# All attention products of an audio tower layer on VectorE, none on GpSimd

## The reference

```python
h = einsum('bnp,dp->bnd', patches, W) + b            # 640 tokens x 512
x = layernorm(h)
q, k, v = x@Wq.T, x@Wk.T, x@Wv.T                     # 16 heads of 32; q, k rotated by position
scores = q k^T / sqrt(32), causal
heavy  = top 10% of the column sums of softmax(scores)   # 1 key of 10
scores = where(heavy | band of width 1, scores, -inf)
h = h + (softmax(scores) @ v) @ Wo.T
x = layernorm(h)
h = h + (silu(x@Wgate.T) * (x@Wup.T)) @ Wdown.T          # inner width 2048
```

## Time and profile before

| what | value |
|---|---|
| median of 3 runs | 337.02 us (336.95 to 338.04) |
| span of the profiled execution | 334.9 us, first to last instruction |
| the median above that span | 2.1 us |
| TensorE busy | 280.9 us (84%) |
| VectorE busy | 210.3 us (63%) |
| GpSimd busy | 157.8 us (47%) |
| mean granted clock of TensorE | 0.946 of full speed (2.4 GHz) |

### The profile page before, as it was taken

One profiled execution on the slowest core, in us unless ns is written; L12 is line 12 of the kernel. 1 busy time (PEld: TensorE's weight loads), 2 busy tenths in 40 slices (PEclk: granted clock), 3 DMA queues, 4 the chain that ended last, 5 costly groups with the idle time before them and its releaser, 6 DMA issues.

```text
span 334.9 us, 4376 instructions
## 1 busy us (share of the span) xinstructions
PE 280.9 (84%) x1528; PEld 247.4 (74%) x1528; DVE 210.3 (63%) x307; ACT 111.8 (33%) x185; POOL 157.8 (47%) x107
## 2 busy tenths in 40 slices
PE   2889689957696898949579998999999999999930
PEld 1468468847585797848469997889999999999920
DVE  4687999999569998598599266554342342342130
ACT  3650110072001544543821033344443443443200
POOL 0656784147847599574599005614223223223100
PEclk9999979989787899989979999999999999999995
DMA  7904777427442054433222202326442433410002
GB/s 251 389 0 95 203 246 179 127 46 206 104 119 94 2 190 145 156 136 125 94 94 94 96 0 80 105 100 225 154 156 94 143 139 94 140 48 0 0 24 70
DMA packets 17602, 39.89 MB, mean 119 GB/s; under 512 B 1908, under 2 KB 10356, under 8 KB 17076
## 3 DMA queue, kind: packets, MB, share of 16 engines
q1 hardware_dynamic: 17588, 39.71, 37.3%
HBM read 34.46 MB, written 5.24 MB: 119 GB/s over the span
## 4 chain that ended last, share of the span: by engine, by line
PE 46%; DVE 28%; issue 9%; ACT 4%; DMA 4%; POOL 3%; SPq 2%; DVEq 0%; ACTq 0%; POOLq 0%
PE ps L201 40%; DVE prod L236 5%; PE ps L1008 4%; DVE hT L847 3%; DVE sm L701 3%; DVE xn L664 2%; POOL wvo L363 2%; DVE pr L729 2%; DVE rstd L661 2%; DVE gu L841 1%; SPq L269 1%; DMA bias_raw<-b_tok 1%; DVE prod L240 1%; DMA regroup<-rot 1%; DVE xT L671 1%
## 5 line engine op out<-in xcount | busy, mean ns | idle before, releaser
L201 PE MATMUL ps<-xT,wgu 128*128 128x256 f32 (+1 forms) x768 | 123.6, 319 | 1.9 <-DVE xT L671 1.8
L201 PEld LDWEIGHTS ps<-xT,wgu 128*128 128x128 f32 x768 | 120.6, 197 | 5.3 <-DVE xT L671 2.5
L363 POOL TENSOR_TENSOR wd<-stage,wd 128x512 fp32r<-128x512 f32 x32 | 52.1, 1631 | 79.2 <-ACT wd L476 79.2
L201 PE MATMUL ps<-wd,hT 128*128 128x512 f32 x240 | 62.7, 403 | 14.6 <-DVE hT L847 13.2
L201 PEld LDWEIGHTS ps<-wd,hT 128*128 128x128 f32 x240 | 44.3, 190 | 24.2 <-DVE hT L847 14.7
L841 DVE TENSOR_TENSOR gu<-silu,ps 128x256 f32<-128x256 f32 (+1 forms) x32 | 15.5, 484 | 62.1 <-PE ps L201 44.2
L363 POOL TENSOR_TENSOR wgu<-stage,wgu 128x1024 fp32r<-128x1024 f32 x16 | 40.0, 2498 | 13.3 <-ACT wgu L476 13.3
L476 ACT ACTIVATE wgu<-stage 128x1024 fp32r<-128x1024 f32 x32 | 33.7, 1055 | 22.8 <-PE ps L201 20.3
L201 PE MATMUL ps<-wvo,xT 128*128 128x512 f32 x120 | 33.6, 439 | 5.1 <-issue 3.2
L847 DVE TENSOR_TENSOR hT<-gu,hT 128x256 fp32r<-128x256 f32 (+1 forms) x32 | 24.3, 759 | 20.5 <-ACT hT L476 20.5
L201 PEld LDWEIGHTS ps<-wvo,xT 128*128 128x128 f32 x120 | 25.2, 215 | 11.9 <-issue 3.3
(11 more groups left out here) (76 smaller groups left out, 270.8 us busy)
## 6 DMA issues: line engine op xcount, KB each, us to landing
stage<-w_ffn SPq DMA_DIRECT2D x32, 768.0 KB, 4.3
regroup<-rot SPq DMA_DIRECT2D x40, 64.0 KB, 2.4
regroup<-v_out SPq DMA_DIRECT2D x20, 64.0 KB, 1.9
stage<-w_k SPq DMA_DIRECT2D x1, 1024.0 KB, 6.4
stage<-w_q SPq DMA_DIRECT2D x1, 1024.0 KB, 8.9
stage<-w_v SPq DMA_DIRECT2D x1, 1024.0 KB, 10.9
stage<-w_o SPq DMA_DIRECT2D x1, 1024.0 KB, 12.9
k_all<-regroup SPq DMA_DIRECT2D x4, 256.0 KB, 2.8
```

The source lines that it names most:

```text
L201: ins = pe.matmul(dst, lhs[a], rhs[b], start=first and n == 0, stop=last and n == 2)
L363: pool.tensor_tensor(dst, src, f32(hi), ALU.subtract).then_inc(done, 1)
```

## The change

The two lists go; every key and value product is made by VectorE, and GpSimd's program has none. The semaphores `score_pool` and `pv_pool` go, and with them VectorE's waits on them. On VectorE the key products (0, 5), (0, 7), (0, 9), (1, 5), (1, 7) are made right before their reductions. The value products are put into its `values` calls: (0, 9) and (0, 8) after (0, 0), ahead of the rotations; (1, 8) after (1, 9), (1, 7) before (1, 6), (1, 4) after (1, 5). TensorE waits on one counter for all of them.

```diff
-POOL_SCORES = [(0, 5), (0, 7), (0, 9), (1, 5), (1, 7)]
-POOL_VALUES = [(0, 9), (0, 8), (1, 8), (1, 7), (1, 4)]
...
@@ GpSimd
             lo_vo(0, 3)
-            scores(0, 5)
-            scores(0, 7)
-            scores(0, 9)
             rotation_sum(6)
             for k in range(KT):
                 lo_vo(1, k)
-            values(0, 9)
             rotation_sum(7)
             rotation_sum(8)
-            values(0, 8)
             rotation_sum(9)
...
             lo_down(0, 0, 0)
-            scores(1, 5)
-            scores(1, 7)
             lo_block(2, 2)
...
-            values(1, 8)
-            values(1, 7)
-            values(1, 4)
             lo_block(12, 0)
@@ VectorE
             def scores(g, i):
-                if (g, i) in POOL_SCORES:
-                    dve.wait_ge(score_pool, POOL_SCORES.index((g, i)) + 1)
-                else:
-                    rotated(dve, g, i)
-                    step(key_products(dve, g, i))
+                rotated(dve, g, i)
+                step(key_products(dve, g, i))
...
-                    if g:
-                        dve.wait_ge(pv_pool, value_number((g - 1, 8)))
...
-            values(0, 5, 4, 3, 2, 1, 0)
+            values(0, 5, 4, 3, 2, 1, 0, 9, 8)
...
-            values(1, 9)
+            values(1, 9, 8)
             up_product(A, 10, 0)
-            values(1, 6)
+            values(1, 7, 6)
             low_product(A, 10, 0)
-            values(1, 5, 3)
+            values(1, 5, 4, 3)
@@ TensorE
-                    pe.wait_ge(pv_pool if (g, i) in POOL_VALUES else pv_dve, value_number((g, i)))
+                    pe.wait_ge(pv_dve, VALUES.index((g, i)) + 1)
```

More of the change, by code:

```diff
@@ L182, in audio_tower @@
         project_mm, rot_read, rot_sum, v_sb = sem("project_mm"), sem("rot_read"), sem("rot_sum"), sem("v_sb")
-        score_pool, score_sum = sem("score_pool"), sem("score_sum")
+        score_sum = sem("score_sum")
         exp_in, exp_out = sem("exp_in"), sem("exp_out")
-        probs, pv_dve, pv_pool, pv_mm = sem("probs"), sem("pv_dve"), sem("pv_pool"), sem("pv_mm")
+        probs, pv_dve, pv_mm = sem("probs"), sem("pv_dve"), sem("pv_mm")
         attn_hi, attn_lo, wo_mm = sem("attn_hi"), sem("attn_lo"), sem("wo_mm")
@@ L242, in value_products @@
                                      repeated(pr[:, i, :, 0:i + 1].rearrange("p h j -> p j h"), 3, HD), ALU.mult)
-        def value_number(item):
-            return sum((k in POOL_VALUES) == (item in POOL_VALUES) for k in VALUES[:VALUES.index(item) + 1])
         def stage_count(p, i, slot):
@@ L386, in rotation_sum @@
                 pool.tensor_tensor(rot[:, n % ROT], rot_cos[:, n % 2], rot_sin[:, n % 2], ALU.add).then_inc(rot_sum, 1)
[L388 to L397, removed]
             def lo_gu(i, slot):
```

## The result

The changed kernel takes 346.33 us (median of 4 executions, 344.73 to 346.95), the kernel before 337.27 (4 executions): a ratio of 1.029, 95% interval 1.024 to 1.034. The span of its profiled execution is 344.6 us against 334.9, 9.7 us longer. The forecast was 345.0.

What follows compares the result with a forecast made beforehand. Bound by a chain of TensorE (46%) and VectorE (28%), with VectorE and GpSimd taking turns in SBUF. 1.5 + 3.8 + 1.0 + 1.7 = 8.0 us on the 334.9 span gives 342.9, median 345.0; range 338.3 to 348.0.

Steps and rivals of the forecast that it cites:

- Group 0: Scores and values ahead of the rotations, made by VectorE alone: first softmax reduction 1.1 us later, `project_out` 1.5 us later.
- Scores of group 1: Products (1, 5) and (1, 7) among GpSimd's low halves in steps 1 to 4: `low_product(3)` 3.8 us later, bounds 0 to 5.
- the two branches: Order at `low_product(2)`, asked within 0.02 us of GpSimd's `lo_gu(5)`: VectorE first, 3.8 us later; GpSimd first, 3.9.
- the rest a turn more: Steps 1 to 4: beyond 2.2 us of own time, (1, 5) and (1, 7) each wait one more turn; 3.8 in all.
- Softmaxes of group 1: Stretch after the group's scores: order and turns of the engines stay as they were, adding nothing.
- Values of group 1: Products (1, 8) and (1, 7) now on VectorE: `low_product(10)` 1.0 us later; (1, 4) free under the value sums.
- The lost turn: Rival at 174.6: GpSimd goes first, so `low_product(10)` is 3.3 us later, not 1.0; total 347.3 us, chance 0.22.
- The clock: TensorE's stall ahead of `down(10)` becomes 2.6 us, its clock falls: 1.7 us more, bounds 0 and 1.7.
- The plain exchange: Rival: new turns cost no more than old, group 1 evens out, only group 0's 1.5 us stays; 338.5 us, chance 0.18.
- The faster one: Rival, steps 1 to 4: low halves fall under VectorE's reductions, 3.3 us of waits go; 335.2 us, chance 0.08.
- it doesn't show: Rival: low clock stretches end where they did and eat the first 1.5 us, the rest evens out; 337.0 us, chance 0.06.
- nothing comes back: Group 1 scores, positions 0 to 3: freed of GpSimd's products, VectorE then waits for the `silu` of step 0; 0 us gained.

Runs made afterwards that it cites:

- the cut of the holding time: GpSimd's gate and up low halves, blocks 2 to 15, first pass, cut from 1024 to 128 columns in both kernels: spans 324.9 us (changed), 322.0 (before).

## Why the prediction was right, and where it wasn't

Counted from the first key product, the forecast's steps against the trace:

| step | forecast | measured |
|---|---|---|
| first softmax reduction later | 1.1 | 1.2 |
| `rotate`, `project_out` later | 1.5 | 1.6 |
| `up_product(0)` to `low_product(3)` longer | 3.8 | 3.8 |
| `low_product(3)` to `low_product(9)` longer | 0 | 0.3 |
| wait for `low_product(10)` longer | 1.0 | 1.1 |
| value sums longer (clock) | 1.7 | 1.6 |
| sum | 8.0 | 8.4 |
| start, before the first key product | - | 0.9 |
| the rest (behind the last matmul) | - | 0.4 |

*Group 0* went as its two sums said: what VectorE takes on is more than the holds it is rid of. Moving two of the products behind `low_attn` gives 2.6 us back at `project_out`, so it was their place ahead of the rotations, not the work, that cost.

*Scores of group 1.* The 3.8 us are what laying the instructions in turns gave. The trace took the second of the two branches, GpSimd ahead of `low_product(2)`, which the forecast put at 3.9 with that low half 5.0 late; it was 4.9 late (counted in the same way, without group 0's part), and the product (1, 8) behind it met no one, 1.35 us. Giving the two products back brought 3.6 us at `low_product(9)` in the trace, and 4.3 of the time. The forecast called the two products' own time 2.2 of the 3.8 and "the rest a turn more"; the cut of the holding time shows that most of even the 2.2 would have found room.

*Softmaxes of group 1.* That the forecast's "nothing" came out as 0.3 us is luck. The fall of the clock behind the stall of 4.64 us made `low_product(4)` end 6.2 us later than in the kernel before, counted from `up_product(0)`; by `low_product(6)` 2.1 of that had come back, 1.3 of it as VectorE waited 2.41 us for the `silu` of step 6 instead of 3.71. In the six traces with all scores of group 1 on VectorE and full low halves, `low_product(3)` to `low_product(9)` took 37.2 to 39.9 us (the kernel before 39.6). So this stretch alone can move the result by over 2 us.

*Values of group 1.* At 174.6 in the forecast's count VectorE and GpSimd were to ask together; VectorE went first, as I took it, but not by a lead: GpSimd's `lo_down(11)` starts at 181.14, (1, 6) at 181.15, with VectorE's (1, 7) just ending. VectorE kept the turn, here and in the six other traces with these products on VectorE. The lost turn didn't come: 1.1 us, not 3.3.

*The clock.* I had nothing but a stall of 1.59 us without a fall and one of 4.30 with one; the 2.66 had one. Filling the stall and giving the values back each brought the 10.21 us back.

*The rivals.* The plain exchange (338.5) needed the new turns to cost no more than the old, and in the steps 1 to 4 they cost 3.8 more. The faster one needed the low halves to fall under the reductions; they fell on three products and two low halves of `hT`. The Trainium skill (Perfetto Trace Analysis, section "Optimizing Scalar/DVE Operations") says that offloading between these two engines might not help, since they share a port; by that the old split might have been worth nothing. This case differs: the split was worth 9 us here, and 1.9 where the early stalls were filled.

*What failed.* The statement that about 0.3% can be told from no change: 35 executions of the kernel before on one chip lay between 333.1 and 339.2 us. And what the early clock does: the rival "it doesn't show" had it eat 1.5 us at most, and I gave it no part in the sum but at the value sums. In the two traces without filling it adds nothing to the difference: `project_out` and the two `gate_up`s take as long in both (8.54 and 8.59 us before, 8.47 and 8.54 after). But it makes VectorE wait for the `silu` of step 0, and in the kernel before that wait hides that GpSimd holds up the product (1, 0): the "nothing comes back" of the forecast held because the clock was low there. With the early stalls filled, the two kernels are 1.9 us apart by their medians, not 9.1. So most of the 9.1 is there only while the clock falls in the early stalls, as far as times from different sittings can show it. The traces with filling are 4.0 us apart, not 9.7. Of these 5.7 us, 1.6 is that the shift of group 0 is gone at `up_product(0)`, 1.5 that the kernel before loses in its steps 1 to 4 by the clock, 1.0 lies between `low_product(3)` and the value sums, 0.4 in the sums, and 1.3 is the start, where the filling has no part. The other 1.5 us by which the medians come together are not accounted for.

## What to carry to other kernels

Where two engines take turns at something, price a move of work by the turns and not by the work: write both instruction streams down in order of asking, and see which low-priority instruction slips in ahead of the one that the next engine waits for. Work that holds the other engine up costs nothing in a stretch in which that engine waits for a third; look for such stretches (here VectorE's 5 us behind `low_attn`) before choosing the engine. A price found this way belongs to the stalls around it: here 9 us became 1.9 once other stalls were filled. And judge a move of a few us by marks within the trace, counted from a common event, when the times of single executions spread as far.

## What the runs showed of the hardware

- VectorE with both operands in SBUF and GpSimd exclude each other for a whole instruction: the cut from 1024 to 128 columns (2.54 to 0.68 us for the same low half) shows it here. At 128.5 GpSimd, which had started 0.08 us earlier, went first; at 181.14 it had started 0.01 us earlier, and VectorE, between two products of its own, went first. The Trainium skill (SBUF — State Buffer, section "Who interferes with whom") says that issue order decides who blocks; the first of these two agrees, the second is too close to tell.
- A granted clock of 1.2 GHz after TensorE stood idle moved the time of the same instructions. The kernel before and its version with the short low halves differ only from block 2 on, but `project_out` took 8.54 and 7.34 us in them and the first two `gate_up`s 8.59 and 6.02 (rows below). At the start of the program, too, matmuls of one form took 0.63 us at 16.84 in the changed kernel and 0.40 already at 13.28 in the kernel before, though the change has no part there. That goes with the 0.9 us in the table; why the start differs stays open.

PE, the first two `gate_up`s of the kernel before, then of its version with the short low halves:

```profile
105.26 8.59 PE L201 MATMUL ps<-xT,wgu 128*128 128x256 f32 x48 [1.41 <-DVE xT L671]
```

```profile
105.14 6.02 PE L201 MATMUL ps<-xT,wgu 128*128 128x256 f32 x48 [1.41 <-DVE xT L671]
```

PE of the changed kernel, then of the kernel before, embedding matmuls:

```profile
16.84 0.63 PE L917 MATMUL ps<-wtok,pat 128*128 128x512 f32 x1
```

```profile
13.28 0.40 PE L950 MATMUL ps<-wtok,pat 128*128 128x512 f32 x1
```
